# Causal attention with ALiBi and a ternary gated MLP on one NeuronCore: weighted sums of three steps in a visit, fifteen probability slots and six key slots, the row of maxima turned later in the first chunk

## The reference, cut to what matters

```python
x = L0_attn_x                                    # (1, 2048, 256), float32, 16 heads of 16
def _L0_attn_ref(x, ...):                        # of the normalised x
    q, k, v = (proj(Wq, bq), proj(Wk, bk), proj(Wv, bv))
    scores = jnp.einsum('bhqd,bhkd->bhqk', q, k) / jnp.sqrt(jnp.float32(HD))
    scores = scores + bias                       # ALiBi: slope of the head * (key - last key)
    scores = jnp.where(causal, scores, jnp.finfo(scores.dtype).min)
    attn = jax.nn.softmax(scores, axis=-1)
    ctx = jnp.einsum('bhqk,bhkd->bhqd', attn, v)
    return ctx @ Wo + bo
def _L0_ffn_ref(x, w1, w2, w3):                  # _bitlinear: weights cut to -1, 0, 1
    hidden = jax.nn.sigmoid(_bitlinear(x, w1)) * _bitlinear(x, w2)
    return _bitlinear(hidden, w3)
x = x + _L0_attn_ref(_layernorm(x), ...)
x = x + _L0_ffn_ref(_layernorm(x), w1, w2, w3)
```

## Time and profile before

| | |
|---|---|
| median of 3 runs | 640.15 us (639.23 to 640.62) |
| profiled execution | 635.68 us, its span 634.0 us |
| PE busy | 592.9 us (94%), 3488 matmuls |
| DVE busy | 462.2 us (73%) |
| ACT busy | 362.2 us (57%) |
| POOL busy | 187.6 us (30%) |
| matmuls of the scores (L1078), turns (L1057), weighted sums (L1091), busy | 245.2, 227.0, 133.3 us |
| bytes moved by DMA | 57.52 MB, 91 GB/s |

### The profile page before, as it was taken

How to read it: one execution, slowest core, us unless ns; L and a number is a source line. 1 busy time by engine, 2 the same in 40 slices (tenths; PEclk the granted TensorE clock), 3 DMA queues, 4 the chain that set the end, 5 groups by cost and what they waited for, 6 DMA issues and landing times.

```text
span 634.0 us, 10885 instructions
## 1 busy us (share of the span) xinstructions
PE 592.9 (94%) x3488; PEld 369.9 (58%) x3488; DVE 462.2 (73%) x1198; ACT 362.2 (57%) x774; POOL 187.6 (30%) x396
## 2 busy tenths in 40 slices
PE   7877788999999999999999999999999999999887
PEld 5554445565667574655656666556555566565487
DVE  5976988577878885677887887888888888311176
ACT  3446447655654456666465464577666674766521
POOL 7636522261341242340212321221200300423300
PEclk9999999999999999999999999999999999999989
DMA  6886743742313126331141130362312110001001
GB/s 193 261 250 169 204 122 86 202 149 72 88 35 102 36 66 202 125 98 38 37 119 34 41 97 2 93 182 77 96 51 69 55 35 1 19 29 43 0 18 34
DMA packets 27453, 57.52 MB, mean 91 GB/s; under 512 B 5316, under 2 KB 14916, under 8 KB 23940
## 3 DMA queue, kind: packets, MB, share of 16 engines
q1 hardware_dynamic: 27396, 56.82, 32.0%
HBM read 40.69 MB, written 14.80 MB: 88 GB/s over the span
## 4 chain that ended last, share of the span: by engine, by line
PE 74%; DVE 16%; issue 5%; ACT 4%; DMA 1%; POOL 0%; ACTq 0%; POOLq 0%
PE pO L1091 20%; PE pS L1078 19%; PE pM L1057 16%; PE pM L1032 5%; DVE pm L1258 5%; DVE pM L1261 3%; PE pM L969 3%; PE pM L1040 2%; ACT probs L895 2%; PE pM L1018 2%; PE pM L977 2%; PE pS L1032 1%; PE pS L969 1%; PE pS L1040 1%; DMA qst<-mT 1%
## 5 line engine op out<-in xcount | busy, mean ns | idle before, releaser
L895 ACT ACTIVATE probs<-pS 128x512 f32<-128x512 f32 (+3 forms) x640 | 300.1, 545 | 171.7 <-PE pS L1078 169.8
L1258 DVE TENSOR_REDUCE pm<-pM 128x1 f32<-128x512 f32 x384 | 239.1, 680 | 46.0 <-PE pM L1057 45.6
L1078 PE MATMUL pS<-qst,kst 128*128 128x512 f32 (+3 forms) x640 | 245.2, 403 | 6.4 <-ACT probs L895 3.8
L1057 PE MATMUL pM<-kst,qst 126*128 126x512 f32 (+3 forms) x640 | 227.0, 384 | 9.3 <-DVE pm L1261 4.2
L1078 PEld LDWEIGHTS pS<-qst,kst 128*128 128x128 f32 x640 | 118.5, 189 | 95.7 <-issue 48.5
L1261 DVE CUSTOM_DVE_ANT_0 pM<-pM,mask 128x128 f32<-128x128 f32 (+3 forms) x256 | 119.7, 522 | 39.7 <-PE pM L1057 39.3
L1057 PEld LDWEIGHTS pM<-kst,qst 126*128 126x128 f32 x640 | 119.6, 190 | 48.6 <-DVE pm L1258 12.7
L775 POOL TENSOR_SCALAR_AFFINE_SELECT probs<-probs 128x128 f32<-128x128 f32 x256 | 77.9, 317 | 218.7 <-ACT probs L895 211.1
L1091 PE MATMUL pO<-probs,vals 128*17 128x512 f32 (+3 forms) x1280 | 133.3, 531 | 0.0
L1091 PEld LDWEIGHTS pO<-probs,vals 128*17 128x17 f32 x1280 | 29.9, 96 | 64.7 <-issue 40.3
L764 POOL CAST hT<-work 128x256 fp32r<-128x256 f32 (+1 forms) x34 | 13.5, 397 | 90.6 <-DVE work L1224 71.3
(11 more groups left out here) (158 smaller groups left out, 424.8 us busy)
## 6 DMA issues: line engine op xcount, KB each, us to landing
kst<-parts SPq DMA_DIRECT2D x78, 256.0 KB
qst<-parts SPq DMA_DIRECT2D x30, 256.0 KB, 4.0
parts<-qk_hl SPq DMA_DIRECT2D x28, 256.0 KB, 4.6
ctx_dram<-ctx_raw SPq DMA_DIRECT2D x15, 256.0 KB, 3.7
xin<-in_L_attn_x SPq DMA_DIRECT2D x5, 512.0 KB, 5.1
out<-work SPq DMA_DIRECT2D x8, 256.0 KB, 4.2
work<-ctx_dram SPq DMA_DIRECT2D x7, 256.0 KB
work<-rden_dram SPq DMA_DIRECT2D x7, 256.0 KB
```

Of the source, the lines that this page charges most:

```text
L895: nc.scalar.activation(probs[:, n % PSLOTS, q0:CH], pS[:, n % SBANKS, q0:CH], ACT.Exp)\
L1057: pe.matmul(max_bank(x)[:, 0:N], qst[0:R_MAX, u % QSLOTS, h, t * P:(t + 1) * P], kst[0:R_MAX, n % KSLOTS, h, 0:N], start=True, stop=True). ...
L1078: pe.matmul(pS[:, n % SBANKS, q0:CH], kst[0:R_END, sl, h, b:b + P], qst[0:R_END, u % QSLOTS, h, q0:CH], start=True, stop=True).then_inc(sc ...
L1258: nc.vector.tensor_reduce(dst, bank, AX.X, ALU.max).then_inc(max_free, 1)
```

## The change

Four things change. The table `visits` says after how many steps PE goes to the weighted sums: 2, 2 in a unit of chunk 0 (as before), 3, 3, 2 in chunk 1, 3, 3, 3, 3 in chunk 2 and 3, 3, 3, 3, 2, 2 in chunk 3. `PSLOTS` goes from 11 to 15 and `KSLOTS` from 7 to 6, which takes the same memory. The swap of units 1 to 4 comes after h = 2 of its step, behind the visit, in place of after h = 0. In the head, the load of w2 is issued before the first `load_m`, its sizes are taken after step 0, those of w3 within step 2, and the second half of a projection group goes ahead of the first swap. With six key slots DVE fills one slot less at the start.

```diff
-    KSLOTS, QSLOTS, PSLOTS, KPOOL = 7, 3, 11, 5
+    KSLOTS, QSLOTS, PSLOTS, KPOOL = 6, 3, 15, 5
...
+    visits = {}
+    for u in range(NU):
+        j = 0
+        for n in {4: (2, 2), 8: (3, 3, 2), 12: (3, 3, 3, 3), 16: (3, 3, 3, 3, 2, 2)}[n_steps[u]]:
+            j += n
+            visits[first_step[u] + j] = n
...
-    swap_in = {first_step[u] - 2: u for u in range(1, NU)}
+    swap_in = {(first_step[u] - 2, 0 if n_steps[u - 1] > TPC else 2): u for u in range(1, NU)}
...
-        return swap_in.get(s) if h == 0 else None
+        return swap_in.get((s, h))
...
             store_parts(("q", 0, 1))
+            load_raw(1, w2)
             load_m(0)
...
             store_parts(Q10)
-            load_raw(1, w2)
...
+                    if (s, h) == (2, SIDE_AFTER):
+                        size_of_weights(2)
...
-                if s in (1, 2):
-                    size_of_weights(s)
+                if s == 0:
+                    size_of_weights(1)
...
+            side_group(Q10, 1)
             swap_max(0)
-            side_group(Q10, 1)
...
-                    if h == 2 and s and s % 2 == 0:
-                        weighted(s - 2)
-                        weighted(s - 1)
+                    if h == 2 and s in visits:
+                        for v in range(s - visits[s], s):
+                            weighted(v)
```

More of the change, by code:

```diff
@@ L1122, in _ @@
                         side_group(side[s])
-                    if h == 2 and s and s % 2 == 0:
-                        weighted(s - 2)
-                        weighted(s - 1)
+                    if h == 2 and s in visits:
+                        for v in range(s - visits[s], s):
+                            weighted(v)
                     if swap_after(s, h):
                         swap_max(swap_after(s, h))
-            weighted(NS - 2)
-            weighted(NS - 1)
+            for v in range(NS - visits[NS], NS):
+                weighted(v)
             pe.wait_ge(probs_ready, G * NS)
```

## The result

The changed kernel took 648.16 us in the median of 4 runs (645.10 to 650.83), the kernel before 640.38 (639.23 to 641.42) beside it: ratio 1.012, 95% interval 1.0063 to 1.0178. It is slower, and outside the range of 630.0 to 643.5. The profiled execution of the changed kernel took 650.21 us, span 648.4.

The account below looks back on a forecast made before the run. PE was taken as the bound, full in chunk 3, with PE and DVE waiting for each other in chunk 0. Terms -6.6 - 0.7 - 5.6 + 8.9 + 1.0 = -3.0 us gave 637.1 us, range 630.0 to 643.5.

Parts of the forecast that it names:

- Fewer visits: On PE: 60 visits to the weighted sums in place of 80, each 0.33 us, saving 6.6 us.
- part of it only uncovers other waits: Bound on the visits' saving on PE: 5 us gained in place of 6.6.
- DVE dry in longer visits: Visits of three steps: DVE fits by only 0.4 us, its other work makes PE wait, +1.0 us.
- Six key slots: Key loads in chunk 3: slots released later, so PE stalls for pieces 28, 29, 30, 33, 34 and 38, +8.9 us.
- The start: Head: DVE's second key slot fill of 1.76 us goes, statistics of x begin earlier, -0.7 us.
- Chunk 0: Late swaps in chunk 0: PE's waits for negated maxima nearly go, DVE wins idle time, -5.6 us.
- The stalls are worse and PE's clock falls: Rival, key load stalls: 11.9 us of stalls and 5.1 of clock, 645.3 us; chance 0.15.
- DVE becomes the bound: Rival, chunks 1 to 3: DVE costs +7 in place of +1, 643.2 us; chance 0.12.
- Carrying the difference: Total: the -3.0 us found on the profiled run, 4.5 us below the median, was applied to the median 640.15.

Follow-up runs that it names:

- e10: Kernel before with a visit of the weighted sums after every step, 160 visits for 80, nothing else changed: 633.10 us, ratio 0.9898.
- e5: Changed kernel with each step's key piece issued ahead of its queries and the last input loads three steps later: 640.81 us, ratio 1.0009.
- e9: e5 with all visits of two steps, 80 visits for 60: 637.90 us, ratio 0.9972.
- e4: Kernel before with six key slots, 15 probability slots and the change's longer visits, without late swap and head edits: 653.33 us, ratio 1.0199.
- e1: Kernel before with six key slots in place of seven and nothing else: 649.51 us, ratio 1.0154.
- e7: e5 with chunk 2 in visits of 3, 3, 2, 2, 2 steps in place of 3, 3, 3, 3: 642.64 us, ratio 1.0020.
- e6: Changed kernel with 28 and 18 transposes of the identity, results unread, ahead of PE's waits for pieces 30 and 33: 644.07 us, ratio 1.0071.
- e3: Kernel before with only the head edits: earlier w2 load, sizes moved, half a projection ahead of the first swap: 638.78 us, ratio 0.9993.
- e2: Kernel before with only the swap of units 1 to 4 moved behind h = 2: 635.62 us, ratio 0.9923.

## Why the prediction was wrong

- **Fewer visits, -6.6.** This step failed, and with it the sign. The price of a visit was right, 0.29 us measured for 0.33; what failed is the step from "PE is full" to "it counts in full". PE is 98% busy in chunk 3 by the average, but the chain of before and of after leaves it for 2.8 us at a unit's end (step 110), where e10's doesn't, and other waits open where visits grow longer. The bound "part of it only uncovers other waits" was set at 5; it should have been open to the other side of nothing. Measured: +3 us for three steps in place of two (2.9 for e5 against e9, 3.8 for e4 against e1, by medians whose intervals overlap), and -7 for one in place of two. With the next term the visits were forecast at -5.6 us and measured +0.5%, some 3 us: that is 8 to 9 of the 11 us between the forecast of -3.0 and the +7.8 measured. What ate the saving of three steps is not the detour of 2.8 us, which is as long with two: up to step 96 it is new waits of PE, 5.2 us in e4 against the 4.0 saved. In chunk 3 a longer wait for DVE comes with them (1.13 us at 549.82, before 0.67 at 531.12); in the unit from step 128 that is part only of the 2.2 us that e5 takes more than e9, and the rest is open.
- **DVE dry in longer visits, +1.0.** The mechanism was there, the place was wrong: I balanced DVE's work against a mean stretch of three steps, not against the last turns before a swap. A wait of its own was missed altogether: with visits after 3, 6, 9 and 12 steps none lies between the swap and the next first score in chunk 2, so the copy to `mT` and its DMA of 2.4 us are bare: 1.36 us at step 60, 1.34 at 96; e7 and e9 took it away, e7 without a gain in chunk 2.
- **Six key slots, +8.9.** Right in kind, near in size. Of the forecast waits, 0.9, 1.7, 3.0, 2.3, 0.4 and 0.6 us, the profile shows 0.65, none, 3.36, 2.18, 0.36 (which it puts down to DVE) and none: 6.6 in all. That of piece 29 went, I take it because PE was at half clock just ahead of it; with six slots alone it is 2.08. What I gave to a rival came on top: the clock, some 4 us by e6, with the doubt said there. Alone this part measured +1.5%, 9.9 us.
- **The start, -0.7.** Not to be told from nothing (-0.1%, interval -0.4 to +0.2). The second memset of 1.76 us is gone, but x arrived at 4.36, so 0.7 us was all that the data allowed. The earlier load of w2, set at nothing or up to 0.5 us, goes with a wait for the first row of maxima that is 0.6 to 0.8 us longer (1.40 in after, 1.52 in e3, 0.76 before).
- **Chunk 0, -5.6.** The size came out, -4.9 by e2's ratio (interval 3 to 7), and the waits at the swaps went as forecast. But at equal clock it is about 3 us, and the sum had no term for the clock here: that the number fits is in part luck. DVE's idle time from 44 to 100 us was to fall by 5 us; it is 9.4 us before, 9.0 after and 10.0 in e2.
- **The rivals.** "The stalls are worse and PE's clock falls" is the one that held, by its consequence more than its cause: the stalls were 6.6 us, not 11.9, and the clock fell three times behind them, 13.6 us at half speed. On the strength of one such case in the trace of before I had given that a chance of 0.15. The rule of the Trainium skill named there ("TensorE: Matmul & The Clock Gate", section "HAM oscillation — how this bites in real kernels") says that waits for DMAs throttle PE again each time, and the traces agree in part. In the profile of after the clock fell at the waits for DMAs of 1.40, 1.34, 3.36 and 2.18 us, but not at that of 1.36 us at 278.43, nor at that of 2.32 us in e4 at 477.40 or of 2.08 us in e1 at 422.14. "DVE becomes the bound" held for the unit ends only. I priced the rivals one by one, each against a forecast with the visits' gain still in it; the result took parts of two and lost that gain.
- **Carrying the difference.** The profiled run of before had spent 3.4 us of its middle at low clock and lay 4.5 us below the median. I carried a difference from one to the other as if both ran alike. Of 79 later runs of that kernel, the 31 with a mean granted clock of 0.980 took 641.92 us in the median, the 2 with 0.994 took 635.84. A typical run thus pays some 5 us more for the clock than the profiled one. Where, that trace can't tell; the profiles of e1, e3 and e4, with mean clocks of 0.976 to 0.987, have the most of it ahead of step 16. One or two us of the swap's gain come from there as well.

## What to carry to other kernels

A busy share of 98% doesn't make an engine's every microsecond count: follow the chain through one whole period, the unit's end with it, and see where it leaves that engine. The price of a burst (0.29 us here) was right and yet decided nothing, so grain is to be tried in both directions; here the finest grain won, with twice the visits of the kernel before: the version with it, the late swap and the start takes 626.74 us. Before a buffer is given up, set each transfer's landing against its first use, with all that is ahead of it in the queue: 7 us of this kernel's time lay in the order of the queue.

## What the runs showed of the hardware

- The granted clock fell to 0.50 behind single waits of 1.34 us (after, 407.60), 2.04 us (e1, 471.33) and 2.18 us (after, 469.55). It stayed at 1.00 behind waits of 2.08 us (e1, 422.14) and 2.32 us (e4, 477.40). So the length of the wait alone didn't decide. The same wait can go either way: the first score of step 60 waits 1.36 us in after and in e5. The row of the score and the window behind it, after and then e5:

```profile
278.43 0.47 PE L1087 MATMUL pS<-qst,kst 128*128 128x512 f32 x1 [1.36 <-DMA qst<-mT]
279.20:282.60 3.40, 3.40 (x33) 1.98 (x32) 2.26 (x4) 1.96 (x5) 1.29 (x1) 1.00 1.01 254
```

```profile
278.65 0.47 PE L1089 MATMUL pS<-qst,kst 128*128 128x512 f32 x1 [1.36 <-DMA qst<-mT]
279.40:282.80 3.40, 3.40 (x20) 1.33 (x22) 2.06 (x3) 1.48 (x3) 1.27 (x1) 0.50 0.94 217
```

- Runs of one kernel differ by the clock: among 79 the time goes from 641.92 us (mean clock 0.980, 31 runs) to 635.84 (0.994, 2 runs) and 636.35 (0.995, 2 runs), and one profiled run shows one of them.
- Filling two waits with transposes nobody reads went with 4.1 us less (e6, medians); behind a third wait, left as it was, the clock stayed up too.
- 80 visits more cost 0.29 us each in the chain of plain steps and yet the kernel was 7 us faster.
